# An adaptive-LN block on one core: LN1 on a transposed copy of x from chunk 4 on

## The reference

```python
h = layernorm(x) * (1 + ca) + sa                  # LN1
omega = clip(softplus(h @ W_omega.T + b_omega), 1e-4, 100)
zeta  = sigmoid(h @ W_zeta.T + b_zeta);  F = h @ W_B.T + b_B
A = omega*omega;  S = 1/(1 + DT*DT*A);  d = 1 - zeta
z, y  = d*(S*z - DT*A*S*y) + F[:M],  d*(DT*S*z + S*y) + F[M:]    # over the 2048 tokens
x = x + ga * (states @ C.T + h @ D_mat.T)
h = layernorm(x) * (1 + cb) + sb                  # LN2
xk = mu_k*h + (1-mu_k)*h_prev;  xr = mu_r*h + (1-mu_r)*h_prev    # one token back
x = x + gb * sigmoid(xr @ W_r) * (relu(xk @ W_k)**2 @ W_v)
```

## Time and profile before

| what | us |
|---|---|
| median of 3 runs | 976.72 (976.17 to 977.73) |
| the profiled execution | 977.14 |
| its span in the profile | 975.4 |
| TensorE busy | 935.9 (96%) |
| VectorE busy | 820.9 (84%) |
| ScalarE busy | 691.5 (71%) |
| POOL busy | 93.5 (10%) |
| DMA, 16 engines, share of time | 20% |

### The profile page before, as it was taken

One profiled execution on the slowest core, in us unless ns is written; L12 is line 12 of the kernel. 1 busy time (PEld: TensorE's weight loads), 2 busy tenths in 40 slices (PEclk: granted clock), 3 DMA queues, 4 the chain that ended last, 5 costly groups with the idle time before them and its releaser, 6 DMA issues.

```text
span 975.4 us, 14746 instructions
## 1 busy us (share of the span) xinstructions
PE 935.9 (96%) x5012; PEld 786.9 (81%) x5012; DVE 820.9 (84%) x2280; ACT 691.5 (71%) x1354; POOL 93.5 (10%) x117
## 2 busy tenths in 40 slices
PE   9995979899999999999999999999999999998997
PEld 3574858788888888888888888888888888887886
DVE  4897779898989989898998979898997989697562
ACT  4979765768777686777868686877768677765451
POOL 0001010001100202010200101110110201000000
PEclk9997998999999999999999999999999999999999
DMA  9820311020211312021121312021131201111001
GB/s 327 280 56 23 109 34 53 12 98 23 87 55 44 99 44 70 18 87 44 57 85 44 98 32 77 23 87 45 44 98 44 98 6 39 44 44 44 23 22 44
DMA packets 35275, 64.78 MB, mean 66 GB/s; under 512 B 3704, under 2 KB 4344, under 8 KB 35200
## 3 DMA queue, kind: packets, MB, share of 16 engines
q1 hardware_dynamic: 35200, 63.84, 19.8%
HBM read 47.02 MB, written 16.81 MB: 65 GB/s over the span
## 4 chain that ended last, share of the span: by engine, by line
PE 83%; DVE 8%; ACT 6%; issue 1%; DMA 1%; DVEq 0%; SPq 0%; ACTq 0%
PE ps_kr L328 32%; PE ps_cd L328 20%; PE ps_tv L328 18%; PE ps_pt L328 7%; PE ps_tv L369 3%; PE ps_pt L336 3%; ACT mix_full L734 1%; DMA stage_out<-in_wd 1%; DVE mix_full L985 1%; PE ps_cd L376 1%; DVE tmp L1206 1%; ACT x_in L600 1%; DVE state L1210 1%; PE ps_tv L389 0%; DVE tmp L1130 0%
## 5 line engine op out<-in xcount | busy, mean ns | idle before, releaser
L985 DVE SCALAR_TENSOR_TENSOR mix_full<-ps_tv,cur_m,mix_full 128x256 f32<-128x256 f32 x256 | 119.1, 479 | 37.7 <-ACT mix_full L734 37.6
L756 ACT ACTIVATE kk<-ps_kr 128x512 f32<-128x512 f32 x64 | 38.1, 599 | 123.4 <-PE ps_kr L328 123.1
L734 ACT ACTIVATE mix_full<-ps_tv,cur_m 128x255 f32<-128x255 f32 x256 | 120.0, 573 | 1.8 <-PE ps_tv L369 1.8
L1484 POOL TENSOR_SCALAR var<-sq 128x2 f32<-128x2 f32 (+1 forms) x34 | 37.1, 1091 | 642.5 <-ACT square_out L582 642.5
L328 PE MATMUL ps_kr<-mix_k_hi,wk_hi 128*128 128x256 f32 x512 | 80.9, 281 | 8.2 <-issue 8.2
L328 PEld LDWEIGHTS ps_kr<-mix_k_hi,wk_hi 128*128 128x128 f32 x512 | 71.2, 191 | 11.2 <-issue 8.8
L328 PE MATMUL ps_kr<-mix_k_hi,wk_lo 128*128 128x256 f32 x512 | 80.1, 279 | 0.0
L328 PE MATMUL ps_kr<-mix_k_lo,wk_hi 128*128 128x256 f32 x512 | 80.0, 279 | 0.0
L328 PE MATMUL ps_kr<-wr_hi,mix_r_hi 128*128 128x512 f32 x256 | 71.5, 402 | 5.5 <-ACT kk L756 5.5
L328 PE MATMUL ps_tv<-wv_hi,kk_hi 128*128 128x512 f32 x256 | 72.8, 408 | 0.8 <-issue 0.8
L328 PE MATMUL ps_kr<-wr_hi,mix_r_lo 128*128 128x512 f32 x256 | 69.9, 395 | 0.0
(11 more groups left out here) (213 smaller groups left out, 2239.6 us busy)
## 6 DMA issues: line engine op xcount, KB each, us to landing
x<-in_x SPq DMA_DIRECT2D x32, 512.0 KB, 3.7
out<-x SPq DMA_DIRECT2D x32, 512.0 KB, 2.8
x_in<-in_x SPq DMA_DIRECT2D x15, 1024.0 KB, 5.1
x<-in_wmod SPq DMA_DIRECT2D x3, 1024.0 KB, 7.6
mix_full<-in_wmod SPq DMA_DIRECT2D x2, 1024.0 KB, 9.1
x_in<-in_x SPq DMA_DIRECT2D x2, 512.0 KB, 5.7
stage_out<-in_wd SPq DMA_DIRECT2D x1, 1024.0 KB, 10.0
stage_mix<-in_wmod SPq DMA_DIRECT2D x1, 1024.0 KB, 10.5
```

The source lines that it names most:

```text
L734: mm = act.activation(mix[n][:, k, 1:UNIT], ps_tv[:, j, c * UNIT:(c + 1) * UNIT - 1], ACT.Identity, bias=cur_m[:, SHIFT + k:SHIFT + k + 1] ...
L756: act.activation(kk[:, i, :], ps_kr[:, i, :], ACT.Relu).then_inc(s_relu, 1)
L985: dve.scalar_tensor_tensor(mix[n][:, k, :], ps_tv[:, j, c * UNIT:(c + 1) * UNIT], cur_m[:, alpha + k:alpha + k + 1], mix[n][:, k, :], ALU. ...
L1484: pool.tensor_scalar(var[:, :], sq[:, :], 1.0 / D, EPS, ALU.mult, ALU.add).then_inc(s_var, 1)
```

## The change

From chunk 4 on (WIDE) LN1 no longer goes through TensorE:

- The host passes a second copy of x, transposed (`xt`). SyncE loads a chunk of it, 512 channels x 512 tokens, straight into h_full.
- x_in is still loaded, now in another order (partition p holds tokens 4p to 4p+3), only for the statistics. ScalarE makes them: `sums1(q+4)` in even units in the place of normalise1, `squares1(q+4)` in odd units ahead of statistics2. VectorE's statistics1 is gone.
- POOL makes rstd1 in the odd unit, ahead of rstd2. SyncE writes rstd and -mean to DRAM (`ln_out`, pieces of 16 bytes), and reads the rstd row back to all partitions (`ln_in`, ln_wide).
- -mean is added to h_full by two accumulating transfers issued by POOL in the next even unit (`centred`), and VectorE multiplies by rstd (`normalised`, two products of 128x1024, L1092 of the new kernel) at the end of that unit. h_blocks then works in place on h_full.
- ScalarE's h_blocks and h_high for blocks 0 and 1 stand behind statistics2. VectorE's h_low of blocks 2 and 3 moves from the end of the odd unit to the next even unit, between read_out and add_out. `take` counts change.
- The big buffers lie at multiples of 2048 bytes in each partition (`to_2048` pads the front). The squares are written as fp32 into buffers that are free, with no waits between them.

```diff
+WIDE = 4
...
+        sb("to_2048", [P, 224])
         proj = [sb(f"proj_{n}", [P, KC, 256], F32R) for n in ("hi", "lo")]
...
+        h = [[sb(f"h_{n}{i}", [P, KC, CHUNK], F32R) for n in ("hi", "lo")] for i in range(2)]
+        xss = [sb(f"xs_{m}", [P, CHUNK], F32R) for m in ("hi", "lo")]
...
+        ln_wide = sb("ln_wide", [P, CHUNK])
...
+        ln_cols = sb("ln_cols", [P, 2, TPC])
+        rstd1, neg_mean1 = ln_cols[:, 0], ln_cols[:, 1]
...
+            def ln_out(q):
+                sp.wait_ge(s_rstd1, q + 1)
+                sp.dma_start(ln_spread[q % 2], ln_cols[:, :, :]).then_inc(s_ln_out, 16)
+            def ln_in(q):
+                sp.wait_ge(s_ln_out, (q - WIDE + 1) * 16)
+                if q > WIDE:
+                    sp.wait_ge(s_z, (q - WIDE) * 2)
+                sp.dma_start(ln_wide[:, :], ln_rows[q % 2, 0:1].partition_broadcast(P)).then_inc(s_ln_wide, 16)
+            def xt_in(q):
+                sp.wait_ge(s_h_lo, q * KC)
+                sp.dma_start(h_full[:, :, :], xt_chunks[q]).then_inc(s_xt, 16)
             for u in range(NUNIT):
...
-                if s % 2 == 1 and u // 2 + 4 < NCHUNK:
+                if u == 1:
+                    sp.wait_ge(s_t1, WIDE * KC)
+                    sp.dma_start(x_in[:, :, :], x_spread[WIDE]).then_inc(s_xin, 16)
+                if s % 2 == 1 and WIDE <= u // 2 + 4 < NCHUNK:
                     q = u // 2 + 4
-                    sp.wait_ge(s_t1, q * KC)
-                    sp.dma_start(x_in[:, :, :], x_rows[q]).then_inc(s_xin, 16)
+                    ln_out(q)
+                    if q + 1 < NCHUNK:
+                        sp.dma_start(x_in[:, :, :], x_spread[q + 1]).then_inc(s_xin, 16)
+                    ln_in(q)
+                    xt_in(q)
...
+            def projections_in(q):
+                if q >= WIDE:
+                    pe.wait_ge(s_pev, q)
+                projections(q)
...
-                        projections(q + 2)
+                        projections_in(q + 2)
                     r_product(u)
                     if u + 2 < NUNIT:
                         cd_product(u + 2)
                 else:
                     if u + 2 < NUNIT:
                         cd_product(u + 2)
-                    if q + 3 < NCHUNK:
-                        t1_first_half(q + 3)
                     r_product(u)
-                    if q + 3 < NCHUNK:
-                        rest_transposed_in(q + 3)
                 v_product(u)
...
-            def squares(x, neg_mean, scratch, out, count, s_sq):
+            def squares(x, neg_mean, spare, out, s_sq):
                 for i in range(out.shape[1]):
-                    if count + i >= 2:
-                        act.wait_ge(s_sq, count + i - 1)
-                    act.activation(scratch[:, i % 2, :], x[:, i, :], ACT.Square, bias=neg_mean[:, i:i + 1],
+                    act.activation(spare[:, i, :], x[:, i, :], ACT.Square, bias=neg_mean[:, i:i + 1],
                                    accum_out=out[:, i:i + 1]).then_inc(s_sq, 1)
             def squares1(q):
                 act.wait_ge(s_mean1, q + 1)
-                squares(x_in, neg_mean1, square_out1, sq1, q * TPC, s_sq1)
+                if q >= WIDE:
+                    spare = x_in
+                else:
+                    act.wait_ge(s_cd, (q - 1) * TPC)
+                    spare = h[q % 2][0]
+                squares(x_in, neg_mean1, spare, sq1, s_sq1)
...
-                squares(x2[:, u % 4], neg_mean2[:, u % 2], square_out2, sq2[:, u % 2], u * TPU, s_sq2)
+                squares(x2[:, u % 4], neg_mean2[:, u % 2], rt if u == 1 else xn2, sq2[:, u % 2], s_sq2)
...
+                    if q >= WIDE:
+                        act.wait_ge(s_z, (q - WIDE) * 2 + 1 + k // 2)
+                        src = h_full[:, k, :]
+                    else:
+                        act.wait_ge(s_t1, q * KC + k + 1)
+                        src = (ps_tv if q == 1 and k >= 2 else ps_pt)[:, k % 2, :]
+                    act.activation(h_full[:, k, :], src, ACT.Identity,
                                    bias=cur_h[:, KC + k:KC + k + 1], scale=cur_h[:, k:k + 1]).then_inc(s_h, 1)
...
+            sums1(4)
+            squares1(4)
...
-                    if next_t1:
-                        normalise1(q + 3)
+                    if q + 4 < NCHUNK:
+                        sums1(q + 4)
                 else:
                     relu_squared(u)
                     if next_mix:
                         mix_high(u + 1, 0)
+                    if q + 4 < NCHUNK:
+                        squares1(q + 4)
+                    if next_cd:
+                        statistics2(u + 2)
                     if next_t1:
                         h_blocks(q + 3, (0, 1))
                         h_high(q + 3, (0, 1))
-                    if next_cd:
-                        statistics2(u + 2)
                     if next_mix:
...
+            def normalised(q):
+                dve.wait_ge(s_ln_wide, (q - WIDE + 1) * 16)
+                for j in range(2):
+                    k = slice(2 * j, 2 * j + 2)
+                    dve.wait_ge(s_centred[j], (q - WIDE + 1) * 16)
+                    dve.tensor_tensor(h_full[:, k, :], h_full[:, k, :],
+                                      ln_wide[:, :].unsqueeze(1).broadcast_to([P, 2, CHUNK]), ALU.mult)\
+                       .then_inc(s_z, 1)
+                    yield
...
                         beside(rec, read_out(u - 1), 2)
+                        if q + 2 < NCHUNK:
+                            beside(rec, h_low(q + 2, (2, 3)), 1)
                         beside(rec, add_out(u - 1), 2)
-                    if next_t1:
-                        beside(rec, statistics1(q + 3), 1)
                     if next_mix:
                         beside(rec, mixes(u + 1), 1)
                     beside(rec, k_low(u), 2)
...
                     run(gated_tanh(u))
                     if next_mix:
                         run(mix_low(u + 1, 1))
-                    take(rec, 1)
                     if next_cd:
                         run(residual(u + 2))
-                    take(rec, 2)
+                    take(rec, 3)
                     out_of_banks = read_out(u)
                     take(out_of_banks, 1)
                     take(rec, 2)
                     run(out_of_banks)
                     if next_cd:
                         beside(rec, normalise2(u + 2), 1)
-                    take(rec, 4)
+                    if next_t1:
+                        beside(rec, normalised(q + 3), 1)
                 else:
                     if s // 2 + 3 == CPB and next_t1:
                         new_columns(b + 1, tab_h, cur_h, s_cur_h)
...
                     if next_cd:
                         beside(rec, normalise2(u + 2), 1)
                     beside(rec, gated_tanh(u), 1)
-                    if next_t1:
-                        beside(rec, h_low(q + 3, (2, 3)), 1)
...
+                if q > WIDE:
+                    pool.wait_ge(s_ln_out, (q - WIDE) * 16)
+                if q != 0 and q != 3:
                     rstd_of(sq1, var1, rstd1, q, s_sq1, s_var1, s_rstd1)
                 else:
...
+                if q >= WIDE:
+                    return
...
+            def centred(q):
+                pool.wait_ge(s_xt, (q - WIDE + 1) * 16)
+                pool.wait_ge(s_ln_out, (q - WIDE + 1) * 16)
+                for j in range(2):
+                    pool.dma_start(h_full[:, 2 * j:2 * j + 2, :],
+                                   ln_rows[q % 2, 1:2].partition_broadcast(P).broadcast_to([P, 2, CHUNK]),
+                                   accum_op=ALU.add).then_inc(s_centred[j], 16)
             rstd2_of(2)
             rstd2_of(3)
+            rstd1_of(4)
             for u in range(2, NUNIT):
                 q = u // 2
-                if u % 2 == 0 and q + 3 < NCHUNK:
-                    rstd1_of(q + 3)
+                if u % 2 == 0 and WIDE <= q + 3 < NCHUNK:
+                    centred(q + 3)
+                if u % 2 == 1 and q + 4 < NCHUNK:
+                    rstd1_of(q + 4)
                 if u + 2 < NUNIT:
...
+        "xt": np.ascontiguousarray(a("attn_u").reshape(B * T, D).T),
```

More of the change, by code:

```diff
@@ L54, in build @@
         wv = [sb(f"wv_{n}", [P, KC, D], F32R) for n in ("hi", "lo")]
+        h = [[sb(f"h_{n}{i}", [P, KC, CHUNK], F32R) for n in ("hi", "lo")] for i in range(2)]
+        xss = [sb(f"xs_{m}", [P, CHUNK], F32R) for m in ("hi", "lo")]
+        with nc.sbuf_tensor("stage_mix", [P, 2, KC, D], F32) as stage_mix:
+            pass
+        mixs = [[sb(f"mix_{n}_{w}", [P, KC, UNIT], F32R) for w in ("hi", "lo")] for n in "kr"]
+        with nc.sbuf_tensor("stage_kk", [P, KC, D], F32) as stage_kk:
+            pass
+        kks = [sb(f"kk_{m}", [P, KC, UNIT], F32R) for m in ("hi", "lo")]
+        with nc.sbuf_tensor("stage_out", [P, KC, D], F32) as stage_out:
+            pass
+        xn2 = sb("xn2", [P, TPU, D])
+        rt = sb("rt", [P, TPU, D])
+        kk = sb("kk", [P, 2, 2 * UNIT])
```

(22 more changed lines are left out.)

12 lines of the change are left out of this document (4 added, 8 removed).

## The result

The changed kernel takes 1002.38 us (median of 4 runs, 1000.26 to 1005.02), the kernel before beside it 977.23 (4 runs): ratio 1.0261, 95% interval 1.0249 to 1.0274. It is slower, as forecast, by 25.1 us where I had forecast 9, and outside the range, which ended at 998. The profiled execution's span is 1000.9.

What follows compares the result with a forecast made beforehand. TensorE was taken to set the pace. Profiled 977.1, +7.8 odd units, +2.5 entry, -1.1 addresses gave 986.3; with the median 0.4 below the profiled execution, 986 us. Range 953 to 998; the forecast's own 980 to 992.

Steps and rivals of the forecast that it cites:

- TensorE's 20.9 us: Chunks 4 to 15: removing 24 transpose pieces of 0.87 us takes 20.9 us of work from TensorE.
- The natural experiment: Unit 26 before the change, already without statistics1: VectorE waits 2.97 us, ScalarE 4.56; taken as model for even units 4 to 24.
- The entry: Ahead of unit 2, ScalarE does sums1(4) and squares1(4): TensorE's wait for xs_lo grows about 2.5 us, bounds 0 and 5.
- neg_mean to the end of tanh: ScalarE, odd unit: 5.2 us as in unit 27, plus 2.5 for h_blocks and h_high moved behind statistics2.
- Transfers and POOL at nothing: New transfers cost nothing; POOL's extra rstd1 is bounded by one 3.65 us hold, of which next to nothing shows.
- rival D: The clock falls behind TensorE's new waits, 3.4 us lost each time; a third of 12 chunks gives +14, 1000; chance 0.07.
- Bounds 0 and -4.5: New buffer addresses: r, v and cd products gain 0.14 us a unit, 4.5 over 32; -1.1 taken, for eight units outside.
- K': The start of an even unit's k_product; times in that unit are counted from it in us.
- 0.2 for two more steps: Even units 4 to 24: two recurrence steps more than unit 26 add 0.2 us to the state's time of K'+17.0.
- K: The start of an odd unit's k_product; times in that unit are counted from it in us.
- The sum for the odd L985: VectorE's first L985 in odd units: 8.57+0.2+2.3-0.6-0.5, given as K+9.95, against K+8.07 before.
- 7.8 forecast for the odd units: Tanh ends at K+26.7, so the next k_product starts later: +0.65 us in each of 12 odd units, 3 to 25.

Runs made afterwards that it cites:

- e4: The changed kernel with eight recurrence steps taken ahead of the mixes in even units from 4 on: 975.96 us.
- e8: e4 with h_blocks and h_high (0,1) put back ahead of statistics2: 966.93 us.
- e3: The changed kernel with nine unused matmuls between r_product and v_product in odd units 3 to 25, filling TensorE's wait for kk_lo: 997.03 us.
- e1: The kernel before with only the buffer order and addresses of the change, both squares sharing one scratch buffer: 979.68 us.
- h1: The kernel before with everything from the mix buffers on moved by 576 bytes, both squares sharing one scratch: 982.57 us.
- e6: e8 with two of squares1's four passes put behind tanh: 991.66 us.

## Why the prediction was wrong

**Right.** That TensorE's 20.9 us would turn into waits; where (ahead of v_product, for kk_lo, in each odd unit); and why (statistics1 had been the filler of VectorE's list, unit 26 shows it). e4 shows it: the place of eight recurrence steps is worth 26 us, the falls of the clock included. The natural experiment was the right witness: L1038 waits 1.8 to 3.0 us, forecast 3; ScalarE waits up to 5.4 for the state, forecast 4.5. The entry, +2.7 for +2.5, though the 4.2 us taken from the earlier trace rows is a wait behind unit 27; the entry's own was 3.3, and became 5.2. normalised, 1.22 us each for 1.15. neg_mean to the end of tanh, 7.65 for 7.7. h_blocks behind statistics2 as the second cause: e8. Transfers and POOL at nothing: VectorE has no wait for them from 200 to 900 us.

The forecast of 9 us failed at three steps, of which no single one makes the difference.

**Wrong, the clock was put at nothing.** The sum priced TensorE's waits as waits only, although it had TensorE waiting 1.7 us at one place and 0.7 at another; the fall of the clock was left to rival D, at 0.07. Measured: the waits add up in one place, 1.5 to 2.4 us, and behind seven of twelve v_product took 7.3 us for 5.7. By e3 that is 6.6 us. D's own price was wrong, too: it took 3.4 us for each fall, half of the 6.9 us of the earlier trace rows, but in 2.0 of these TensorE was still waiting, and here tanh hides a part; a fall cost 0.9. That D's 1000 lies near the measured 1002 is luck. A wait once predicted should have been priced at both clock levels.

**Wrong, k_product.** "Bounds 0 and -4.5" for the addresses excluded a loss for no reason. I had looked at the stationary operand's start alone, and k_product was the fast one only in the old place. It costs 0.28 us in each unit (e1, h1), 9 us over 32, against some 6 that r, v and cd gain; in the chain it delays ScalarE, too, as every relu comes 0.28 later (L1038 at K'+8.35 for 8.07).

**Mis-sized, the chain from the even unit to tanh.** "0.2 for two more steps": from the first L1038 to the state it took 9.8 us in unit 16 and 9.4 on average, in unit 26 of the trace before 8.9. With k_product's 0.28, unit 16's Ln came at K'+29.2 and not 28.3, kk_lo at K+21.1 and not 20.4, tanh at K+27.4 and not 26.7. With the clock held up (e3) the odd units are 27.23 on average, 1.24 longer than before, where I had 0.65: 7 us over twelve. About half of it is k_product, by an estimate: the state is 0.6 later than forecast on average (K'+17.8 for 17.2), and 0.28 of that is k_product's. No run separates the two. (The sum for the odd L985 in the prediction gives 9.97 and not 9.95, which changes nothing.)

Together: 7.8 forecast for the odd units, +7.1 by the chain, +6.6 by the falls is the measured 21.5. The even units' 1.7 and the 2.1 behind unit 26 (+1.0 where I had -1.1) are for the most part k_product: e1, with the addresses alone, has 1.4 and 0.7 there.

## What to carry to other kernels

When work that nobody waits for is taken from an engine's hand-ordered list, look at what was interleaved with it: here statistics1's place held nine steps of a serial chain, and without it they came after a wait instead of before. A wait put on TensorE is to be priced twice, with the matmuls behind it at the full and at the lower clock. Before moving a piece on one engine, read every list that consumes it, the helper engine's, too: in e6 two squares moved on ScalarE held up an unrelated rsqrt on POOL, and the kernel was 25 us longer. And where a large change loses a little everywhere, reordering the free engines is worth more than undoing it: from 1002 to 958 us with no operation removed.
